# Narrow attention in steps of four key chunks: order of maxima, scores and weighing, and a new share-out of the PSUM banks

## The reference, cut to what matters

```python
def _L1_xattn_ref(queries, keys, values, valid_lens, Wq, Wk, Wv, Wo):   # D = 256, H = 16
    q = split_heads(queries @ Wq)       # (b, 16, 256, 16)
    k = split_heads(keys @ Wk)          # keys = values = the context, (b, 16, 4096, 16)
    v = split_heads(values @ Wv)
    scores = jnp.einsum('bhqd,bhkd->bhqk', q, k) / jnp.sqrt(jnp.float32(hd))
    mask = jnp.arange(skv)[None, None, None, :] < valid_lens[:, None, None, None]
    scores = jnp.where(mask, scores, NEG)
    p_attn = jax.nn.softmax(scores, axis=-1)
    out = jnp.einsum('bhqk,bhkd->bhqd', p_attn, v)
    return out.transpose(0, 2, 1, 3).reshape(b, sq, D) @ Wo
```

## Time and profile before

| | |
|---|---|
| Median of three runs | 4065.47 us (4065.18 to 4066.49) |
| The profiled execution | 4062.29 us, span 4060.4 us |
| PE busy (matmul) | 3559.6 us, 88% of the span |
| DVE, ACT, POOL busy | 61%, 56%, 41% |
| Narrow attention, main loop | 2581 to 3516 us |

### The profile page before, as it was taken

The page is one execution under the profiler, slowest core; times in us unless marked ns, Lnnn a source line. Parts: engine busy times, 40 slices in busy tenths (PEclk is TensorE's granted clock), DMA queues, the critical chain, the costliest instruction groups (busy, mean ns, idle before and its releaser), DMA issues. The chain is left out here.

```text
span 4060.4 us, 81430 instructions
## 1 busy us (share of the span) xinstructions
PE 3559.6 (88%) x30262; PEld 2601.7 (64%) x30262; DVE 2494.8 (61%) x3852; ACT 2289.3 (56%) x4294; POOL 1663.4 (41%) x1365
## 2 busy tenths in 40 slices
PE   5899999999999999998677985799999877677399
PEld 3687778877787878886445984455555443333298
DVE  5666666666666666663274112678787877367587
ACT  3566666666666666667152112466666666345165
POOL 2577777777777777777032002110101000024033
PEclk9899999999999999999787997899999999789599
DMA  6777677776777766662203566778788744000011
GB/s 221 269 274 272 250 271 270 276 279 252 269 270 274 263 256 237 238 245 92 83 8 134 206 242 200 196 177 171 176 170 178 140 66 64 15 11 1 21 48 42
DMA packets 231719, 723.30 MB, mean 178 GB/s; under 512 B 47372, under 2 KB 128524, under 8 KB 162444
## 3 DMA queue, kind: packets, MB, share of 16 engines
q1 hardware_dynamic: 228640, 709.70, 54.9%
q0 software_dynamic: 2688, 8.39, 0.6%
HBM read 623.61 MB, written 94.37 MB: 177 GB/s over the span
## 5 line engine op out<-in xcount | busy, mean ns | idle before, releaser
L801 POOL TENSOR_TENSOR wa_acc<-wa_acc,wa_probs 128x512 f32<-128x512 f32 x960 | 1258.4, 1311 | 478.4 <-ACT wa_probs L647 365.7
L714 DVE TENSOR_REDUCE wa_mx<-wa_ps_x 128x1 f32<-128x512 f32 x1024 | 658.5, 685 | 363.3 <-PE wa_ps_x L500 363.2
L647 ACT ACTIVATE wa_probs<-wa_ps_s 128x512 f32<-128x512 f32 x1024 | 530.3, 602 | 546.1 <-PE wa_ps_s L543 545.7
L1340 DVE TENSOR_REDUCE na_mx<-na_ps_m 128x2 f32<-128x1024 f32 x512 | 613.8, 1220 | 195.5 <-PE na_ps_m L1161 192.0
L1285 ACT ACTIVATE na_probs<-na_ps_s 128x512 f32<-128x512 f32 x1024 | 555.9, 594 | 309.4 <-PE na_ps_s L1181 307.0
L639 ACT ACTIVATE wa_ps_s<-wa_m_wide 128x512 f32<-128x512 f32 x1024 | 578.4, 614 | 0.0
L521 PE MATMUL wa_ps_o<-wa_probs,wa_values 128*64 128x256 f32 x4096 | 468.9, 382 | 0.0
L521 PEld LDWEIGHTS wa_ps_o<-wa_probs,wa_values 128*64 128x64 f32 x4096 | 285.6, 137 | 158.4 <-ACT wa_probs L647 23.6
L465 PE MATMUL wa_ps_x<-wa_k_ctx,wa_w_k 128*128 128x512 f32 x1488 | 380.2, 403 | 5.7 <-DMA wa_k_ctx<-ctx_split 5.3
L488 PE MATMUL wa_ps_x<-wa_w_v,wa_v_ctx 128*128 128x256 f32 x2880 | 364.1, 284 | 0.0
L488 PEld LDWEIGHTS wa_ps_x<-wa_w_v,wa_v_ctx 128*128 128x128 f32 x2880 | 357.3, 191 | 5.9
(11 more groups left out here) (345 smaller groups left out, 5739.2 us busy)
## 6 DMA issues: line engine op xcount, KB each, us to landing
wa_k_ctx<-ctx_split SPq DMA_DIRECT2D x248, 1024.0 KB, 7.0
wa_v_ctx<-ctx_split SPq DMA_DIRECT2D x120, 1024.0 KB, 8.1
na_ctx<-ctx_split SPq DMA_DIRECT2D x56, 1024.0 KB, 11.4
na_keys<-k_rows SPq DMA_DIRECT2D x384, 128.0 KB
ctx_split<-wa_stage SPq DMA_DIRECT2D x32, 1024.0 KB, 5.0
wa_land<-in_ctxT SPq DMA_DIRECT2D x32, 512.0 KB, 11.5
ge_w_b<-in_w_rows SPq DMA_DIRECT2D x8, 2048.0 KB
k_rows<-na_k_high SPq DMA_DIRECT2D x64, 256.0 KB, 2.8
```

What stands on the lines that cost most here:

```text
L647: act.activation(probs[:, c % R:c % R + 2, h * SQ:(h + 1) * SQ], ps_s[n % BANKS][:, :].rearrange("p (c n) -> p c n", c=2), ACT.Exp).then_i ...
L714: dve.tensor_reduce(mx[:, half, h, k:k + 1], ps_x[banks[h]][:, :], AX.X, ALU.max).then_inc(m_taken, 1)
L801: pool.tensor_tensor(to[:, :], to[:, :], probs[:, c % R, :], ALU.add).then_inc(summed, 1)
L1340: dve.tensor_reduce(mx[:, half, :, k], ps_m[n % 2][:, :, :], AX.X, ALU.max).then_inc(m_taken, 1)
```

## The change: what it does

The main loop of a pair gets 8 steps of four chunks (`SS = CH // 4`). A step on PE is: the maxima of one half of the queries, the scores of four chunks, the maxima of the other half, and then either one projection (a whole half, in steps 0, 2, 4 and 6) or the weighing (step 1: one group of four chunks, steps 3 and 5: two, step 7: three). The scores get four banks, two steps t deep. The other three banks, `ps_x`, are shared by the maxima, the projections (always bank 1) and the turned maximum (bank 0). Each head's maximum product is reduced by an instruction of its own (128x512). The maxima of block k of pair a + 1 come in step k - 1 of pair a. The sums of a pair are added up inside `ps_o`, copied to SBUF by ACT (`take_sums`), and divided on DVE once for two pairs (64 partitions), in step 3 of every second pair; the output of two pairs is stored at once. In the prologue the maxima of pair 0 use the three banks, the values use two of the score banks, and the first maxima of pair 1 are put before pair 0.

```diff
+        def max_block(a, st):
+            pair, k = (a + 1, st + 1) if st < SS - 1 else (a + 2, 0)
+            return (pair, k) if pair < G else None
+        def reductions(a, st):
+            return 4 * min((a + 1) * SS + st + 1, G * SS)
+        def maximum_banks(st, half):
+            return ((0, 1), (2, 0))[half] if st % 2 == 0 else ((2, 0), (1, 2))[half]
+        def item(a, st):
+            if st % 2:
+                return None
+            n = k_block(a) if st < 4 else v_block(a)
+            return None if n is None else ("keys" if st < 4 else "values", n, st % 4 // 2)
+        WEIGHED = {1: (0,), 3: (1, 2), 5: (3, 4), 7: (5, 6, 7)}
...
-        ps_s = [s.ps(f"ps_s{i}", [P, 512]) for i in range(2)]
-        ps_m = [s.ps(f"ps_m{i}", [P, 2, 512]) for i in range(2)]
-        ps_p = s.ps("ps_p", [P, 512])
+        ps_s = [s.ps(f"ps_s{i}", [P, 512]) for i in range(4)]
+        ps_x = [s.ps(f"ps_x{i}", [P, 512]) for i in range(3)]
...
# tensor, scores and add_up
-                pe.wait_ge(exp_done, 1 + n)
+                if n >= 2:
+                    pe.wait_ge(exp_done, 1 + 2 * (n - 1))
...
-                pe.matmul(ps_p[0:W, 0:SQ], sel_num[:, :], ov[:, :], start=True, stop=True)
-                pe.matmul(ps_p[0:W, SQ:2 * SQ], sel_den[:, :], ov[:, :], start=True, stop=True).then_inc(summed, 1)
+                pe.matmul(ps_o[r:r + W, 0, :], sel_num[:, :], ov[:, :], start=True, stop=True, tile_position=(0, r))
+                pe.matmul(ps_o[r:r + W, 1, :], sel_den[:, :], ov[:, :], start=True, stop=True, tile_position=(0, r)
+                          ).then_inc(summed, 1)
...
+            def first_maxima(a, k):
+                n = 4 * (a * SS + k)
+                if a:
+                    pe.wait_ge(q_ready, 1 + 2 * a)
+                if n:
+                    pe.wait_ge(m_taken, 1 + n)
+                maximum(a, k, 0, maximum_banks(1, 0))
+                pe.wait_ge(m_taken, 1 + n + 1)
+                maximum(a, k, 1, maximum_banks(1, 1))
...
# tensor, main loop (the old loop over t is removed)
             turn_maximum(0)
+            first_maxima(1, 0)
             for a in range(G):
+                for st in range(SS):
+                    of_max, taken = max_block(a, st), reductions(a, st)
+                    if of_max is not None:
+                        if st == 0:
+                            pe.wait_ge(q_ready, 1 + 2 * (a + 1))
+                        pe.wait_ge(m_taken, 1 + taken - (st % 2 == 0))
+                        maximum(*of_max, 0, maximum_banks(st, 0))
+                    scores(a, 2 * st)
+                    scores(a, 2 * st + 1)
+                    if of_max is not None:
+                        before = item(a, st - 1) if st % 2 else None
+                        if before is not None and before[0] == "keys":
+                            pe.wait_ge(masked, 1 + 2 * before[1] + before[2] + 1)
+                        elif before is not None:
+                            pe.wait_ge(v_ready, 1 + 2 * before[1] + before[2] + 1)
+                        pe.wait_ge(m_taken, 1 + taken + 1)
+                        maximum(*of_max, 1, maximum_banks(st, 1))
+                    if st == 0 and a:
+                        add_up(a - 1)
+                    if item(a, st) is not None:
+                        kind, n, part = item(a, st)
+                        pe.wait_ge(m_taken, 1 + taken + 2)
+                        if kind == "keys":
+                            project_keys(n, part, ps_x[1])
+                        else:
+                            project_values(n, part, ps_x[1])
+                    if st == SS - 1 and a + 1 < G:
+                        pe.wait_ge(m_taken, 1 + taken + (2 if of_max is not None else 0))
+                        turn_maximum(a + 1)
+                    for u in WEIGHED.get(st, ()):
+                        weigh(a, u)
             add_up(G - 1)
...
# scalar
+            def take_sums(a):
+                r = W * (a % 2)
+                act.wait_ge(summed, 1 + a + 1)
+                if a >= 2:
+                    act.wait_ge(o_ready, 1 + a // 2)
+                act.activation(sums[r:r + W, :, :], ps_o[r:r + W, :, :], ACT.Copy).then_inc(sums_ready, 1)
...
+                for st in range(SS):
+                    for h in range(2):
+                        exponents(a, 2 * st, h)
+                    if st in (1, 3) and kb is not None:
+                        take_high(kb, st // 2)
+                    for h in range(2):
+                        exponents(a, 2 * st + 1, h)
+                    if st == 0 and a:
+                        take_sums(a - 1)
+                    if st in (4, 6) and vb is not None:
+                        take_values(vb, st // 2 - 2, ps_x[1])
+                    if st == SS - 1 and a + 1 < G:
+                        take_maximum(a + 1)
...
# vector
-                dve.tensor_reduce(mx[:, half, :, k], ps_m[n % 2][:, :, :], AX.X, ALU.max).then_inc(m_taken, 1)
+            def take_maxima(a, k, st):
+                n = a * SS + k
+                for half in range(2):
+                    dve.wait_ge(m_done, 1 + 2 * n + half + 1)
+                    for h in range(2):
+                        dve.tensor_reduce(mx[:, half, h, k:k + 1], ps_x[maximum_banks(st, half)[h]][:, :], AX.X, ALU.max
+                                          ).then_inc(m_taken, 1)
...
+                for st in range(SS):
+                    if st == 0 and a:
+                        copy_out(a - 1)
+                    if max_block(a, st) is not None:
+                        take_maxima(*max_block(a, st), st)
+                    if st == SS - 2 and a + 1 < G:
+                        finish_maximum(a + 1)
+                    if item(a, st) is not None and item(a, st)[0] == "keys":
+                        mask_keys(*item(a, st)[1:], ps_x[1])
+                    if st == 3 and a % 2 == 0 and a:
+                        divide(a - 2)
...
# sync: the store of two pairs' output comes after the stores of the keys
-                if a:
-                    store_out(a - 1)
                 if k_block(a) is not None:
                     store_keys(k_block(a), 0)
                     store_keys(k_block(a), 1)
+                if a % 2 == 0 and a:
+                    store_out(a - 2)
```

More of the change, by code:

```diff
@@ L951, in narrow_attention @@
         ov = s.sb("ov", [P, SQ])
-        rden = s.sb("rden", [W, SQ])
-        o_sb = [s.sb(f"o_sb{i}", [W, SQ]) for i in range(2)]
-        ps_s = [s.ps(f"ps_s{i}", [P, 512]) for i in range(2)]
-        ps_m = [s.ps(f"ps_m{i}", [P, 2, 512]) for i in range(2)]
-        ps_p = s.ps("ps_p", [P, 512])
+        sums = s.sb("sums", [2 * W, 2, SQ])
+        rden = s.sb("rden", [2 * W, SQ])
+        o_sb = s.sb("o_sb", [2 * W, SQ])
+        ps_s = [s.ps(f"ps_s{i}", [P, 512]) for i in range(4)]
+        ps_x = [s.ps(f"ps_x{i}", [P, 512]) for i in range(3)]
         ps_o = s.ps("ps_o", [P, 2, SQ])
@@ L1008, in narrow_attention @@
             loads[True, n] = loads[False, n]
-        def first_bank(n, half):
-            return ps_m[1][:, 0, :] if half == 0 and n < 4 else ps_p
         @block.sync
@@ L1116, in _, with project_keys @@
                     store_keys(k_block(a), 1)
-            store_out(G - 1)
-            for i in range(2):
-                sp.wait_ge(o_stored[i], 1 + 16 * (G // 2))
+                if a % 2 == 0 and a:
+                    store_out(a - 2)
+            store_out(G - 2)
+            sp.wait_ge(o_stored, 1 + 16 * (G // 2))
         @block.tensor
         def _(pe):
-            def project_keys(n, m, bank, parts=range(KD)):
+            def project_keys(n, m, bank):
                 i = buffer(n, False)
-                if m == 0 and 0 in parts:
+                if m == 0:
                     pe.wait_ge(ctx_in[i], 1 + 16 * loads[False, n])
-                for c in parts:
+                for c in range(KD):
                     for x, (w, of) in enumerate(((w_high, 0), (w_high, 1), (w_low, 0))):
@@ L1214, in _ @@
                 for half in range(2 if n < CG else 0):
-                    pe.wait_ge(v_ready, 1 + (2 * n + half if n >= 4 else max(2 * n + half - 1, 0)))
-                    project_values(n, half, first_bank(n, half))
+                    pe.wait_ge(v_ready, 1 + max(2 * (n - 1) + half + 1, 0))
+                    project_values(n, half, ps_s[2 + half])
                 if n >= 5:
-                    maximum(0, 2 * (n - 5))
-                    maximum(0, 2 * (n - 5) + 1)
-            for u in range(2 * (FIRST - 5), ST):
-                maximum(0, u)
+                    first_maxima(0, n - 5)
+            for k in range(FIRST - 5, SS):
+                first_maxima(0, k)
             turn_maximum(0)
+            first_maxima(1, 0)
             pe.wait_ge(masked, 1 + 2 * FIRST)
@@ L1383, in _ @@
                 if n >= 5:
-                    take_maximum(0, 2 * (n - 5))
-                    take_maximum(0, 2 * (n - 5) + 1)
-            for u in range(2 * (FIRST - 5), ST):
```

(24 more changed lines are left out.)

123 lines of the change are left out of this document (33 added, 90 removed).

## The result

The changed kernel takes 4121.25 us (median of four runs, 4114.49 to 4121.69), the kernel before took 4065.98 (four runs, 4065.18 to 4066.52). The ratio is 1.0128, with a 95% interval of 1.0113 to 1.0143: slower by 1.3%, some 55 us. Forecast were 4100 us, 35 more than before, with a range of 4045 to 4135. The profiled execution took 4121.36 us, its span is 59.1 us above that of before (4060.4).

What follows compares the result with a forecast made beforehand. It took the one-score-bank loop (1.67 us a step) to bound the kernel before, then the maxima chain. Pairs with both projections +38.4, other pairs 1.1, 3.8, 0.2, pair 0 5, tail 0.6, last pair -14: +35, 4100 us; range 4045 to 4135.

Steps and rivals of the forecast that it cites:

- What is late next? The maxima.: Main loop: with the score loop gone, PE and DVE wait for each other within each step over three shared banks.
- The step prices: Pair's eight steps: even 3.15 us, step 1 2.77, steps 3 and 5 3.65, step 7 5.25; sum 27.9 us.
- the projections: Pairs with projections: keys add 0.5 us in step 2 and 1.3 in step 0, both halves of values 0.7.
- rival A: Maxima to reductions: hand-over below 0.49 us, not 0.54; pairs of 29.3 and 26.8 us, total 4057 us; chance 0.12.
- four exponential pairs: ACT in a step of four chunks: they take 2 us, 16 us a pair, so ACT no longer limits.
- Edits at nothing: ACT's sums copy (0.6 us, in idle time), earlier key stores, later output store and POOL's work: no cost.
- rival C: Key stores queued behind context loads come too late, holding DVE 2 us a pair: 4140 us; chance 0.07.
- B: Rival: first maxima and reductions run without gaps, DVE's work bounds a pair at 23 us; 3920 to 3960; chance 0.12.
- D: Rival: a full score bank still holds PE up, periods stay 27.7 to 28.9 us, time within 0.2%; chance 0.04.
- Head and tail: Stage ends: pair 0 ends 5 us later (bounds -2 and +8), last output 0.6 more, last pair gains 14.
- six late pairs x 0.63 = 3.8: Late pairs without projections: 0.63 us more each than before, 3.8 us for six.
- the 0.4 for each pair with values alone: Pairs projecting values only: 29.1 us against 28.7 before, three pairs costing 1.1 us.

Runs made afterwards that it cites:

- experiment 4: The changed kernel with two score banks in place of four, the other two idle: 4358.7 us, one run.
- experiment 5: The changed kernel with each maximum reduction taking only the first 256 of its 512 columns: 4007.3 us, one run.
- experiment 2: The changed kernel with last-batch weighings spread, one group in each of steps 1 to 6 and two in step 7: 4091.95 us, ratio 1.0073.
- experiment 1: The changed kernel with the division of two pairs moved from step 3 to step 7: 4101.0 us, ratio 1.0085.
- Experiment 3: The changed kernel with six unused matmuls in steps 2, 4 and 6 of pairs without a projection: 4115.8 us, ratio 1.0127.
- experiment 9: The kernel before, with the projections' bank as head 0's second score bank in the last batch: 4056.6 us, ratio 0.9992.
- 11: The kernel before with four last-pair score banks, and in pairs 24 to 30 a third, head 0's next scores ahead of the weighing: 4035.6 us, ratio 0.9934.

## Why the prediction was right, and where it was short

**The mechanism.** *What is late next? The maxima.* So it is. The trace has the waits of PE for DVE over `ps_x` (182.8 us) and none of weight for exponentials; experiment 4 brings the old loop back with the banks, experiment 5 takes 3 us out of a pair by shortening the reductions, and experiment 2 shows that a weighing behind an odd step's second maximum costs its length on the chain. The gap of 0.60 us on DVE before an odd step's first reduction is there as well (at 3402.54 and 3408.42), and the one at the pair's end, 2.04 us.

**The step prices.** At full clock 3.17, 2.71, 3.57 and 5.01 us stand against 3.15, 2.77, 3.65 and 5.25. Four even steps, one of 2.71, two of 3.57 and one of 5.01 are 27.5 us against the 27.9 forecast; experiment 1 has three late pairs of 27.5 without a fall. The division costs 1.0 in every second pair against 0.95 (experiment 1). The row of experiment 1 gives 30.34 for a pair with both projections and no division; with 0.5 for the division that is 30.85, against 30.9 forecast. Inside that sum two small errors cancel, which is luck: the pair by itself was 0.4 us too dear on paper (27.9 for 27.5), the projections 0.3 too cheap (2.5 for 30.34 - 27.5 = 2.8). Twenty of these pairs were to cost 38.4 us and cost 38.3 where the clock held. The forecast's own terms give 39.0 for them and 36 for the whole, 1 more than it wrote; rival A's would be nearer -11 than -9. Its "four exponential pairs" in a step are four instructions, two pairs, at 2.06 us.

**Edits at nothing.** ACT's copy of the sums takes 0.59 us (0.6 was taken) and no engine waits for it:

```profile
L1310 ACT ACTIVATE na_sums<-na_ps_o x20: 586/588/590, 2627.4 to 3216.9; 32x512 f32<-32x512 f32 x20
```

No wait for a key store shows, so rival C did not occur. Splitting the reductions was priced at 1.0 to 1.4 us of DVE time a pair. The whole profile page has 613.8 us for them before, in 512 instructions, and 659.0 in 1024 after, so 45.2 / 32 = 1.4:

```profile
L1340 DVE TENSOR_REDUCE na_mx<-na_ps_m 128x2 f32<-128x1024 f32 x512 | 613.8, 1220 | 195.5 <-PE na_ps_m L1161 192.0
```

That is at the upper end, and below the 2.0 us estimated from the figure of the Trainium skill (Perfetto Trace Analysis, Optimizing Scalar/DVE Operations): 0.09 us for each extra instruction in place of 0.125. DVE's whole busy time grew less, from 239.8 / 300 x 28.95 = 23.1 us a pair to 253.0 / 330 x 31.07 = 23.8, because the division now comes once for two pairs.

**The rivals.** A needed a hand-over below 0.49 us and periods of 29.3: no pair with projections is below 30.3. B needed first maxima and reductions without gaps; the windows above have DVE 77% busy. D is experiment 4's kernel, not this one.

**Head and tail.** Pair 0 and the prologue cost 7.9 us, at the upper bound of 8: PE waits for pair 1's keys until 2590.38 and then runs at half clock up to 2598. The last pair takes 23.2 us, between the 21 and 26 us that the forecast named for full and half clock, and gains 12.2; ACT's stalls behind double weighings are there, one of 0.95 us at full clock and one of 2.51 after the clock fell:

```profile
3561.94 4.03 ACT L1296 ACTIVATE na_probs<-na_ps_s 128x512 f32<-128x512 f32 x8 [0.95 <-PE na_ps_s L1193]
...
3568.47 4.03 ACT L1296 ACTIVATE na_probs<-na_ps_s 128x512 f32<-128x512 f32 x8 [2.51 <-PE na_ps_s L1193]
```

**The step that was mis-sized** is *six late pairs x 0.63 = 3.8*, together with the 0.4 for each pair with values alone. It took full clock for granted. At full clock the late pairs would have cost less still: 27.5 + 0.5 - 27.73 = 0.3 us each, 1.8 for six. They cost 16.7, so some 15 us are the clock, with 6 more in three of pairs 1 to 20 and a few in pairs 21 to 23 and 30. Experiment 3 bears this out: with the same weighings and the clock at 0.99, pairs 24 to 30 take 29.1 us in place of 30.6, fillers included. The forecast used the low clock for the two ends of the stage and did not ask what PE's new waits would do to it in the middle, though it worked out even steps with a long wait for DVE (1.38 us in the rows above) and two weighings in a row in the odd ones. The busy share alone would not have told it. In the late pairs of the kernel before, PE was busy for 75% of the time, less than the 79% after, and the clock was full:

```profile
3309.00:3420.00 111.00, 83.17 (x944) 41.47 (x944) 87.89 (x89) 72.03 (x137) 2.43 (x8) 1.00 0.50 68
```

PE's gaps of over a quarter of a us there were 0.9 us long, six in a pair, with one of 1.3 at the turn; after the change most are 0.3 us, and some three in a pair 1.4. The median is 21 us above the forecast. The falls cost somewhat more than that; the 5 us by which the untouched stages were shorter hide a part of it.

**What stays open**: which divisions are followed by a fall and which are not, in code that is the same, and what in PE's work decides it in the late pairs. Fillers end the falls there and the division's place ends them in pairs 1 to 20, but neither the share of idle time nor a gap of 1.33 us is enough by itself. The spread of the times does not help: the six executions of experiment 2 lie between 4087.75 and 4102.74 us, and eleven of the kernel before on the same chip between 4055.34 and 4073.60, though its profiled execution has no fall from 2604 to 3481 us.

## What to carry to other kernels

When banks are shared out anew, write down the whole ring that remains, with the order of the in-order engine in it: a bank that comes free helps only if the next instruction for it does not stand behind another (experiment 9 against 11), and work behind a producer that is waited for costs its length, while the same work in a waiting gap costs nothing (experiment 2). Use freed banks where they lie idle, as in the last pair, before taking them from a loop that is balanced. And where a change puts new waits of over 1 us on TensorE ahead of long bursts, name the low clock on these bursts as a risk with a price, even if the mean busy share is no lower than before.

## What the runs showed of the hardware that was not expected

In the changed kernel the clock falls in the middle of a busy stage, for 3.4 or 6.8 us at a time, while PE's busy share over hundreds of us is about 80% (253.98 of 320 us at a mean clock of 0.89, above). In the pairs with both projections each fall came behind a gap of PE that the division had made (1.33 us at 3104.93, fall at 3106.7), but most gaps of this kind were followed by none. In the late pairs no division is needed: the falls at 3379.8 and 3386.6, for example, have only the usual 1.38 us waits of the even steps ahead of them. A double weighing takes 1.92 us at the full clock and 3.04 to 3.61 in a fall. Matmuls with no use in the gaps held the clock at 0.99 and made the pairs shorter by 1.3 us although they lengthened their steps (experiment 3). The Trainium skill (TensorE: Matmul & The Clock Gate, A second HAM failure mode: psum-queue depth-cycling) tells of another kernel whose matmuls went through banks in turn, idled briefly between groups and so swung between the two levels. The late pairs of the changed kernel agree (clock 0.89, the gaps above); those of the kernel before also idle between groups, for a larger share of the time, and stay at 1.00. Moving one 2 us division on another engine ended the falls in the 20 pairs with both projections, in three profiled executions of three.
